# Feed-forward: a signal from the middle of TensorE's gate and up product, and the first half of new weights split from there on

## What is computed

```python
logits = x @ router_w                       # 8192 tokens, 32 experts, 8 chosen for each
xs = jnp.repeat(x, K, axis=0)[sort_idx]     # rows sorted by expert
gate = ragged_dot(xs, w_gate, group_sizes)  # 1024 -> 512 for each expert
up   = ragged_dot(xs, w_up, group_sizes)
down = ragged_dot(silu(gate) * up, w_down, group_sizes)   # 512 -> 1024
routed = (down[unsort].reshape(T, K, H) * tkw[..., None]).sum(axis=1)
shared = silu(x @ sw_gate) * (x @ sw_up) @ sw_down        # 1024 -> 1024 -> 1024
out = x + routed + shared
```

## Time and profile before

| | us |
|---|---|
| median of 3 runs | 13982.54 |
| the profiled execution | 13916.77 |
| its span | 13915.1 |
| TensorE busy in it | 13460.4 |
| feed-forward, first to last matmul | about 2370 to 13902 |

### The profile page before, as it was taken

The page is one execution under the profiler, slowest core; times in us unless marked ns, Lnnn a source line. Parts: engine busy times, 40 slices in busy tenths (PEclk is TensorE's granted clock), DMA queues, the critical chain, the costliest instruction groups (busy, mean ns, idle before and its releaser), DMA issues.

```text
span 13915.1 us, 195311 instructions
## 1 busy us (share of the span) xinstructions
PE 13460.4 (97%) x59424; PEld 10927.4 (79%) x59425; DVE 6480.4 (47%) x7111; ACT 3094.5 (22%) x4072; POOL 6447.4 (46%) x6981
## 2 busy tenths in 40 slices
PE   9999995999999999999999999999999999999999
PEld 7888884888888787887877777787888887887887
DVE  6888885333333333334333334334333334666666
ACT  4444441111111212112121222212111111111111
POOL 6778885333333333333333333333333334555554
PEclk9999997999999999999999999999999999999999
DMA  3444444333333433334333434434333334777777
GB/s 123 117 111 117 114 113 85 94 111 111 94 110 110 126 110 124 93 112 142 96 108 107 129 122 144 139 99 153 94 93 111 94 93 128 250 247 244 250 251 237
DMA packets 935880, 1846.00 MB, mean 133 GB/s; under 512 B 168913, under 2 KB 515921, under 8 KB 909474
## 3 DMA queue, kind: packets, MB, share of 16 engines
q0 software_dynamic: 318976, 892.19, 20.1%
q1 hardware_dynamic: 132898, 599.04, 14.0%
q10 hardware_dynamic: 483840, 352.54, 9.5%
HBM read 1261.41 MB, written 597.54 MB: 134 GB/s over the span
## 4 chain that ended last, share of the span: by engine, by line
PE 78%; DMA 2%; DVE 2%; issue 1%; ACT 0%; DVEq 0%; ACTq 0%; SPq 0%; POOL 0%; POOLq 0%
PE gps L1343 26%; PE ups L1343 26%; PE yps L1343 25%; DMA hsd<-hb 1%; DVE wlo L1254 1%; DMA hz<-hsd 0%; DMA raw<-in_w_gu_dram 0%; DVEq L1053 0%; DVE xlo L1254 0%; ACT xhi L1200 0%; DVE hp L1297 0%; ACT whi L1194 0%; ACTq L1206 0%; DVE yrow L1285 0%; ACTq L1053 0%
## 5 line engine op out<-in xcount | busy, mean ns | idle before, releaser
L1126 POOL DMA_INDIRECT xg<-xnd,xidx x2688 | 2734.1, 1017 | 1204.4 <-issue 632.8
L1166 POOL DMA_INDIRECT yd<-yrow,yidx x544 | 578.9, 1064 | 4707.8 <-DVE yrow L1316 4684.2
L1254 DVE TENSOR_TENSOR xlo<-xt,xhi 128x1024 fp32r<-128x1024 f32 x672 | 822.7, 1224 | 3997.1 <-ACT xhi L1200 3996.6
L1343 PE MATMUL gps<-whi,xhi 128*128 128x512 f32 x5376 | 2133.6, 397 | 213.1 <-DVE xlo L1254 131.8
L1343 PE MATMUL gps<-wlo,xhi 128*128 128x512 f32 x5376 | 2129.3, 396 | 0.0
L1343 PE MATMUL gps<-whi,xlo 128*128 128x512 f32 x5376 | 2128.9, 396 | 0.0
L1343 PE MATMUL ups<-whi,xhi 128*128 128x512 f32 x5376 | 2127.8, 396 | 0.0
L1343 PE MATMUL ups<-wlo,xhi 128*128 128x512 f32 x5376 | 2127.3, 396 | 0.0
L1343 PE MATMUL ups<-whi,xlo 128*128 128x512 f32 x5376 | 2126.7, 396 | 0.0
L1343 PE MATMUL yps<-whi,hhi 128*128 128x512 f32 x5376 | 1701.7, 398 | 117.1 <-DVE wlo L1254 96.8
L1343 PE MATMUL yps<-wlo,hhi 128*128 128x512 f32 x5376 | 1697.9, 397 | 0.0
(11 more groups left out here) (168 smaller groups left out, 17539.3 us busy)
## 6 DMA issues: line engine op xcount, KB each, us to landing
hsd<-hb ACTq DMA_DIRECT2D x2688, 64.0 KB
hz<-hsd ACTq DMA_DIRECT2D x672, 256.0 KB
raw<-in_w_gu_dram SPq DMA_DIRECT2D x136, 1024.0 KB, 7.3
raw<-in_w_dn_dram SPq DMA_DIRECT2D x68, 1024.0 KB, 6.7
kT<-in_ctx_dram SPq DMA_DIRECT2D x64, 704.0 KB, 8.6
xg<-xnd,xidx POOLq DMA_INDIRECT x2688
xin<-in_x_dram SPq DMA_DIRECT2D x64, 512.0 KB
thi<-kph SPq DMA_DIRECT2D x64, 512.0 KB, 5.9
```

What stands on the lines that cost most here:

```text
L1126: pool.indirect_dma_start(out=xg[slot][:, q, :], out_offset=None, in_=quarters, in_offset=bass.IndirectOffsetOnAxis(ap=xidx[slot][:, q:q + ...
L1166: pool.indirect_dma_start(out=yd, in_=yrow[i][:, :], in_offset=None, out_offset=bass.IndirectOffsetOnAxis(ap=yidx[i][:, 0:1], axis=0), bou ...
L1254: return dve.tensor_tensor(dst, src, hi.bitcast(F32), ALU.subtract)
L1343: ins = pe.matmul(ps, rows, w[:, chunk, i * 512:(i + 1) * 512], start=first and n == 0, stop=last_one and n == 2)
```

## The change

TensorE gets a new semaphore `gu_half`: the last matmul on chunk 3 of 8 adds to it, when units 0 and 1 of gate and up weights are done with. ScalarE and VectorE get a second branch on F_FIRST ahead of `x_high(t+1)` and `x_low(t+1)`; in it they split units 0 and 1 of the next expert (ScalarE after a wait on `gu_half`). The branch that stood there splits units 2 and 3 alone. SyncE, GpSimd and the matmuls are as they were.

In ScalarE's `tile(c)`:

```diff
                 if c.on(1):
+                    if c.part(-1) != 1:
+                        with act.If(entry(act, c.n(1), F_FIRST, 1) == 1):
+                            act.wait_ge(gu_half, t + 1)
+                            split_gu(entry(act, c.n(1), F_EXPERT, NE - 1), range(GU // 2))
                     x_high(c.n(1))
...
                         with act.If(entry(act, c.n(1), F_FIRST, 1) == 1):
-                            split_gu(entry(act, c.n(1), F_EXPERT, NE - 1))
+                            split_gu(entry(act, c.n(1), F_EXPERT, NE - 1), range(GU // 2, GU))
```

In VectorE's:

```diff
                 if c.on(1):
+                    if c.part(-1) != 1:
+                        with dve.If(entry(dve, c.n(1), F_FIRST, 1) == 1):
+                            split_gu(entry(dve, c.n(1), F_EXPERT, NE - 1), range(GU // 2))
                     x_low(c.n(1))
...
                         with dve.If(entry(dve, c.n(1), F_FIRST, 1) == 1):
-                            split_gu(entry(dve, c.n(1), F_EXPERT, NE - 1))
+                            split_gu(entry(dve, c.n(1), F_EXPERT, NE - 1), range(GU // 2, GU))
```

In TensorE's:

```diff
                         last = three(xhi[:, m, :], xlo[:, m, :], m, (gps[:, :], ups[:, :]),
                                      m == 0, m == KX - 1)
+                        if m == KX // 2 - 1:
+                            last.then_inc(gu_half, 1)
                     last.then_inc(gu_mm, 1)
```

More of the change, by code:

```diff
@@ L1044, in feed_forward @@
         gidx_ready, yidx_ready = sem("gidx_ready"), sem("yidx_ready")
-        gu_mm, down_mm = sem("gu_mm"), sem("down_mm")
+        gu_half, gu_mm, down_mm = sem("gu_half"), sem("gu_mm"), sem("down_mm")
         x_turned, h_turned, h_st, h_ld = sem("x_turned"), sem("h_turned"), sem("h_st"), sem("h_ld")
@@ L1183, in _, with split_gu @@
         def _(act):
-            def split_gu(e):
-                for q in range(GU):
+            def split_gu(e, units=range(GU)):
+                for q in units:
                     act.wait_ge(w_ld[q], 16 * (e + 1))
```

## The result

The changed kernel takes 14023.28 us (median of 7 runs, 14012.39 to 14032.76), the kernel before 13982.54 beside it (7 runs, 13975.52 to 13989.77): a ratio of 1.0029, 95% interval 1.0017 to 1.0040. It is slower by 41 us, where +15 was forecast; that lies inside the range, but on the other side of the 0.2% line from the likeliest class.

A forecast was written before the change was run, and what follows sets the result against it. TensorE, busy for 97% of the span, bounds the kernel, so only its waits can be won. Terms -7, +8, +12, +5.5 and -4 give +15 us, median 13982.5 to 13997, range 13960 to 14047.

The forecast's parts named there:

- ordinary changes: Changes of expert away from short experts, 13 counted: TensorE's 1.34 us idleness goes, late hlo leaves -0.5 us each.
- no harm: Rival: loads leave the exchange of h as it was, hhi about 10 us after xhi; -47 us, 13936; chance 0.07.
- the queues take turns: Rival: stores wait as at tile 60, hz only 3.3 us, hhi at 13.65; -21 us, 13961; chance 0.06.
- The slower rival: Rival: hz waits as in the row of 8.34 us, hhi at 18.7; +64 us, 14047; chance 0.29 for above +28.
- The start of hhi: Load of h's high part after xhi: stores at 4.1, hz at 10.3, hhi at 16.35 us instead of 9.60.
- the 21 tiles like tile 60: Experts' second tiles, where stores of h meet two down loads: 5.7 to 7.0 us to hz, 6.2 in the middle.
- second changes: Seven changes of expert one tile after another: xhi stands behind late hhi and split, TensorE waits about 2.8 us on hp.
- Single ones: Four one-tile experts standing alone: the next down load comes later behind late hhi; +2.0 us each, 8 in all.
- Threes: Three pairs of one-tile experts in a row, a third change following: xhi behind the second unit; +4.0 us each, 12 in all.
- The pair 238 and 240: Changes around a two-tile expert: at 240 TensorE starts 0.6 later, hlo 2 later, about 2 us lost; +1.5 together.
- tile 608: Last change of expert, no loads after it: low parts made early let VectorE reach hlo sooner; -4 us.
- The group of 144: Changes at tiles 144 to 147: at 147 four units load while h goes out, about 3.5 us lost; +5.5 together.

The follow-up runs named there:

- second: The changed kernel, but SyncE issues no gate and up load before the low part of unit 2 is made: 13896.42 us, ratio 0.9989.
- third: The changed kernel, but loads of units 2 and 3 wait for the low part of unit 3, those of 0 and 1 stay early: 13901.04 us, ratio 0.9995.
- fourth experiment: The changed kernel, but one unit instead of two split early and no load before the second low part: 13867.23 us, ratio 0.9969.
- the two repeats: The changed kernel itself run twice more, unaltered: 13998.03 us, ratio 1.0018, and 14014.02 us, ratio 1.0029.
- the experiments with waits of 1.90 and 2.63 us: One unit split early, loads as before, hhi of an expert's last tile held, with one or nine tiny ScalarE activations: 14033.76 and 14070.87 us, one execution each.
- late-after-short kernel: The changed kernel, but after a one-tile expert units 0 and 1 are split in their old place: 13985.17 us, ratio 1.0023.
- experiments 1: The changed kernel with its new branch and wait on gu_half kept, but all four units split in the old place: 13909.18 us, ratio 1.0000.
- 5: The changed kernel, but one unit instead of two split early, with SyncE's loads not held: 13935.71 us, ratio 0.9974.
- the last: One unit split early instead of two, no load before the second low part, run again on another chip: 13932.63 us, ratio 0.9971.

## Why the prediction was right, and where it wasn't

**The mechanism holds.** The wait on low parts before gps is gone, and the exchange of h pays: the stores and hz meet loads that used to come after them. With the loads held back in whole or in part (second, third and fourth experiment), at least ten of the twelve ordinary changes give their 1.6 us. The branch is free, as said. The rivals "no harm" (-47) and "the queues take turns" (-21) fall: hhi starts at 16.8 after xhi on median, not near 10 or 13.65. The slower rival (+64) falls too at its own row: hz takes 7.3, not 8.34, on median.

**The start of hhi** was forecast at 16.35 and came at 16.76 on median (16.43 and 16.71 in the two repeats), but three terms inside it are off. The stores go out at 4.5 after xhi, not 4.1, since ScalarE takes longer to issue past the branch: the first high part starts 4.5 ahead of xhi, not 4.9. The wait from stores to hz is 4.95, not 6.2: the 21 tiles like tile 60 were the nearest rows, and they are 1.2 too long. hz to hhi is 7.3, not 6.0: the two rows of 6.55 and 8.34 stood behind four loads, and I had taken less because two of these are missing here. It took as long without them. In the traces of all kernels what stands behind hz counts for nothing, and what stands just ahead of it for everything (last section). The errors cancel nearly, which is luck, not foresight. hlo ends at 18.1, not 17.75, and 18.3 was the point from which an ordinary change gives nothing back. With that the 12 ordinary changes were to give -0.5 each and gave between -1.1 and +3.9.

**The sum had no term for the clock.** Each wait was costed at its own length. Before, nearly all waits at ordinary changes are the 1.34 us, and behind none of those the clock falls. The change puts uneven ones in their place, 0.5 to 4.1 us at 19 of the 20 changes that don't follow a short expert (1.7 in the middle, where 1.1 was forecast), and mostly 3.4 to 3.8 us at second changes; behind most of those of 2 to 4 us it does (15 of 18 waits between 1.95 and 4.4 us in this trace). That is +23.2 of the +42.7, and the experiments with waits of 1.90 and 2.63 us, which differ in the wait alone, show that it takes no more than the wait. By the prediction's own prices hhi at 16.76 would have made the sum +23, and the waits came to +19.5.

**The terms one by one.** Ordinary changes: -6 forecast, waits +3.0, clock +7.9. Nearly all of the loss is at tiles 208, 325, 386 and 416, where hhi of the tile before came 17.1 to 18.7 after the zero and the clock fell. In the repeats the same twelve come to -7.2 and +0.8, so this term is hardly worth its sign. Single ones: +2.0 each forecast, +2.2 measured (1.6 waits, 0.6 clock). The step behind this price holds, if somewhat larger than forecast: the down load after the second change was to come 38.6 us after the first zero instead of 36.6, and it came after 39.0 to 40.3. Threes: +4.0 forecast and measured, but the size is right for the wrong reason: 1.7 each are waits and 2.3 clock. The wait at a second change is 3.4 to 3.8 us, at one of the seven 2.3 (2.8 forecast), at a third 15.4 to 15.8 (about 18 forecast). The pair 238 and 240: +1.5 forecast, +3.8 measured (5.3 and 5.8 in the repeats); tile 608: -4 forecast, -2.1 measured. The group of 144: +5.5 forecast, +11.6 measured, the term that was missed most. Its waits are +7.5 and its clock +4.2.

**The rule on packets.** That a DMA engine takes turns between its queues (the Trainium skill, page "DMA: Bandwidth & Descriptors", section "Queues, rings and completion order") would have given hz some 3.3 us. At the 19 changes it took 7.3, and 2.5 with no load under way. As a bound on how long a small transfer waits behind two large ones the rule fails. And one load issued level with hz costs it some 3 us where one issued 0.14 us after it costs nothing: the order of issue decides, which turns alone don't say. Why wasn't found.

**What would have been better.** The row to look for was in the trace of before: behind its long waits at short experts the matmuls are slow for a while, 28.5 us in all. Had I looked at how the matmuls start after each kind of wait, I would have added some 2 us for each new wait over 3 us, the 7 second changes first.

**Still open.** The loss of the same kernel's profiled feed-forward went from +24.5 to +42.7, mostly at ordinary changes, tile 544 among them; I don't know what sets hhi early or late there, since hz takes anything from 5.7 to 8.7 us in the three traces of this kernel. Why the clock falls behind one wait of 2.63 us and not behind another wasn't found. In the groups of three the late-after-short kernel gained less than half of what the theory says, and why wasn't tried. Why two ordinary changes, 325 and 544, often don't give their 1.6 us wasn't looked into either. And the 12 us before a down product after each one-tile expert stand in all versions.

## What to carry to other kernels

Work moved earlier moves everything that waits for its buffers: before moving a step, list the transfers that its end sets free, and put them beside the small transfers that the critical path waits for. Move by the smallest unit that removes the wait: here one unit ahead of the silu gives back all 1.6 us at nearly every ordinary change, and the second only brings its loads into the way of h. Where a small transfer of the critical path and a large one are issued at about the same moment, see to it that the small one goes first by more than a tenth of a microsecond, by a semaphore if need be (not tried here). Cost a wait of TensorE with what comes after it: up to 2 us it costs its length, from 3.3 us on its length and some 2 more, so many short waits can be cheaper than a few middling ones.

## What the runs showed of the hardware

How long the 256 KB load of hz takes, from its issue to hhi, goes by hundredths of a microsecond. In the six kernels that issue it about level with a 1 MB load on SyncE's queue (before and experiments 1, 2, 4, 5 and the last), at the 19 changes each:

```
1 MB load issued      0.13 to 0.18   0.09 to 0.13   0.05 after      0.08 to 0.77
against hz            after it       after it       to 0.02 ahead   ahead of it
changes               29             25             52              8
hz to hhi, us         2.4 to 3.5     4.0 to 5.1     5.4 to 6.1      4.8 to 5.5
```

The loads that follow the first one 0.5 to 2.3 us later make no difference. With one load 1.1 to 2.6 us ahead of hz and the next between 0.4 ahead and 1.1 behind, as the changed kernel has it, it is 5.7 to 8.7 (57 changes in three traces, 7.3 in the middle). In the late-after-short kernel the next one comes 1.1 to 2.1 behind at 18 of the 19, and it is 4.4 to 5.8. I had expected a smooth sum of what is left to drain.

Four stores of h behind two 1 MB loads take 4.9 us until hz can be issued, against 3.2 free.

The fall of the granted clock behind an idle TensorE isn't a threshold on the length of that one wait: 2.63 us brought it about half of the time, and below 1.95 us once in 206.

The first low part behind a read of the table and a branch comes 0.8 to 0.9 us late on VectorE, 1.9 behind two nested ones (tile 207 of the late-after-short kernel); enough to move a load from one side of a collision to the other.
